# Two-layer graph network: the chain from aggregation to scores in 20 slots instead of 23

## The chip, the cores and the metric

The kernel runs on one core of one Trainium2 chip (trn2). The metric is the device time of one execution in microseconds. The kernel before took 729.9 us (median of 3 runs, 729.87 to 730.22).

## The reference

4096 nodes with 256 features and a 4096 x 4096 adjacency matrix go through two layers, each with a residual and a layer norm. The first averages neighbours and combines them with the node itself. The second scores every pair of a node and a neighbour with small tanh networks, masks the scores, takes a softmax over each row and averages values with it.

```
mask = adj > 0;  deg = mask.sum(1)
agg  = mask @ x / max(deg, 1)
out  = relu(concat(x @ W_self + b_self, agg @ W_nb + b_nb) @ W_comb + b_comb)
x1   = layernorm(x + out)
neib_att = tanh(neigh @ Wn1 + bn1) @ Wn2 + bn2
value    = neigh @ Wv + bv
x_att    = tanh(x1 @ Wx1 + bx1) @ Wx2 + bx2
ws   = softmax(where(mask, leaky_relu(x_att @ neib_att.T), NEG_BIG), axis=1)
out2 = concat(x1 @ Wfx + bfx, ws @ value)
return layernorm(x1 + out2)
```

## The kernel before

The rows are handled in 32 blocks of 128 nodes (`NB`), and the neighbours of a block in 8 groups of 512 (`NG`, `GW`). Each engine has its own instruction list, and all lists are written by one loop over slots, `for s in range(0, SLOTS + 3)`. A slot is no time but a place in the order. Block b begins its aggregation in slot 8b; `due(s, at)` says which block and group has a step with offset `at` in slot s, and `due(s, at, 0)` is for steps done once a block. Block 31 aggregates in slots 248 to 255. At any time work of five blocks is interleaved. Engines wait on each other by semaphores only.

Products are made with numbers split into a high and a low 16-bit half; so each step that feeds a matmul is a high half on ScalarE and a low half on VectorE, which subtracts.

The chain of a block, with its offset from slot 8b:

- masks (`make_mask`, VectorE, from `adj_sb`, in four quarters, at the offsets `MASK_SLOTS`), then SyncE's queue turns each quarter with a transposing DMA into `mask_t` (`turn_mask`) and loads the next block's quarter of adj (`load_adj`). `mask_t` has one buffer; the turn of a quarter waits for the aggregation of the same quarter of the block before.
- 0 to 7: `aggregate` on TensorE, one group a slot. 8: `degrees` (VectorE), `mean_of` (ScalarE). 9: `mean_transpose` (TensorE). 10: `mean_high`. 11: `mean_low`. 12: `combine` (TensorE, 12 matmuls of 256 columns). 13: `layer0` (four VectorE instructions) and `norm1` (three GpSimd ones). 15: `normalise1` gives `x1`. 16: `x1_transpose`. 17 and 18: `x1_high`, `x1_low`. 19: `hidden_and_fx`. 20: `x_tanh`, `tanh_low`. 21: `x_attention`. 22: `xatt_high`, `xatt_low`, which fill `stack`, and `add_fx`.
- 23 to 30: `scores` (TensorE, one group a slot) and `leaky` (ScalarE), one slot later `masked_scores` (VectorE). 31: `row_max`. 32 to 36: `exps`, four quarters. 33 to 38: `turn_p`, transposes of the exponentials of six groups on TensorE, each followed by `p_high` and `p_low`; the other two groups are split by `wide_high` (35) and `wide_low` (36) and turned by DMA (37). 34 to 41: `weigh_values`, 12 matmuls a slot. 42: `layer1`, then `norm2`, `normalise2` and the store.

Score matmuls use two PSUM buffers, so `scores` of a group waits for `leaky` of two groups earlier; so does `turn_p` for `p_low`. `weigh_values` of a block's first group waits for the third step of `layer1` of the block before, since `ps_v` has one buffer.

The list of SyncE has, in each slot, in this order: wide turn, mask turn with adj load, `turn_x` (offset 4), the x load (`LAYER0_AT + 1`) and the store. Slots 0 to 11 also hold the last preparations: values and attention parts of neighbour tiles 4 to 7, and splitting of x (`first_part`). After slot 255 there is no aggregation and the list drains until slot 289.

Of the kernel before, what the change touches and what calls it, by code (L numbers as in the profile page):

```python
# [50 lines left out]

MASK_SLOTS = (-7, -5, -1, 0)
MEAN_AT = 8
MEAN_T_AT = 9
MEAN_SPLIT_AT = 10
MEAN_LOW_AT = 11
X_TURN_AT = 4
COMBINE_AT = 12  # L60
LAYER0_AT = 13
X1_AT = 15
X1_T_AT = 16
X1_COPY_AT = 17
X1_LOW_AT = 18
HIDDEN_AT = 19
TANH_AT = 20
XATT_AT = 21
STACK_AT = 22
SCORE_AT = 23  # L70
ROW_MAX_AT = 31
TURN_AT = 33
WEIGH_AT = 34

# [2 lines left out]
BY_PE = NG - 2 * BY_DMA  # L79
EXPS = ((0, 1), (1, 0), (2, 2), (4, 3))  # L80
EXP_PLACE = [[quarter for _, quarter in EXPS].index(k) for k in range(4)]
WIDE_HIGH_AT = (35,)
WIDE_LOW_AT = (36,)
WIDE_TURN_AT = (37,)
WIDE_WEIGH_AT = (40,)
LAYER1_AT = 42
SLOTS = NG * (NB - 1) + LAYER1_AT + 1


# [6 lines left out]
def due(s, at, k=None):  # L96

    b, g = divmod(s - at, NG)
    return (b, g) if 0 <= b < NB and (k is None or g == k) else None
# [19 lines left out]
def gnn_kernel(nc, x, adj, w_self, b_self, w_nb, b_nb, w_comb, b_comb, neigh, wx1, bx1, wx2, bx2,  # L119
# [5 lines left out]
    with ExitStack() as ctx:  # L125
# [362 lines left out]
        def _(dve):  # L488
# [207 lines left out]
            def row_max(b):  # L696
                dve.wait_ge(score_made, NG * (b + 1))
                dve.tensor_reduce(row[:, 0:1], part_max[:, :], AX.X, ALU.max).then_inc(max_step, 1)
                dve.wait_ge(max_step, 2 * b + 1)
                at_least(dve, exp_made, NQ * (b - 1))  # L700
                dve.tensor_scalar(exp_bias[:, b % 2:b % 2 + 1], row[:, 0:1], minus_unit, EXP_SHIFT, ALU.mult,  # L701
                                  ALU.add).then_inc(max_step, 1)

            def degrees(b):
                dve.wait_ge(agg_done, NQ * (b + 1))
                at_least(dve, mean_made, b)
                dve.tensor_scalar(row[:, 4:5], ps_agg[b % 2][:, D:D + 1], EDGE_F8, x_scale, ALU.max,
                                  ALU.mult).then_inc(degree_step, 1)
                dve.wait_ge(degree_step, 2 * b + 1)
                dve.reciprocal(row[:, 5:6], row[:, 4:5]).then_inc(degree_step, 1)  # L710
# [32 lines left out]
            def xatt_low(b):  # L743
                s = slice(H, 2 * H)
                dve.wait_ge(xatt_hi, b + 1)
                dve.scalar_tensor_tensor(out=stack[s, b % 2, :], in0=ps_x[s, 0:P], scalar=bx2_sb[s, 0:1],  # L746
                                         in1=stack[s, b % 2, :], op0=ALU.add, op1=ALU.subtract).then_inc(stack_ready, 1)

            def add_fx(b):
                dve.wait_ge(resx_made, b + 1)  # L750
                dve.scalar_tensor_tensor(out=res[:, b % RES_BUFS, 0:DV], in0=ps_x[:, 3 * P:4 * P], scalar=fx_inv,
                                         in1=res[:, b % RES_BUFS, 0:DV], op0=ALU.mult, op1=ALU.add).then_inc(res_made, 1)

            def p_low(b, j, n):
                dve.wait_ge(p_hi_made, n + 1)
                dve.tensor_tensor(p_lo[:, n % 2, :], ps_t[n % 2][:, :], p_hi[:, n % 2, :],  # L756
                                  ALU.subtract).then_inc(p_lo_made, 1)
# [23 lines left out]
            for s in range(0, SLOTS + 3):  # L781
                first_part(s)
                if d := due(s, LAYER1_AT, 0):
                    layer1(d[0])
                if d := due(s, SCORE_AT + 1):
                    masked_scores(*d)
                if d := due(s, MEAN_AT, 0):
                    degrees(d[0])
                if d := due(s, MEAN_LOW_AT, 0):
                    mean_low(d[0])  # L790
                if d := due(s, X1_LOW_AT, 0):
                    x1_low(d[0])
                if d := due(s, TANH_AT, 0):
                    tanh_low(d[0])
                if d := due(s, ROW_MAX_AT, 0):
                    row_max(d[0])
                if d := due(s, LAYER0_AT, 0):
                    layer0(d[0])
                if d := due(s, STACK_AT, 0):
                    xatt_low(d[0])  # L800
                    add_fx(d[0])
                for q, at in enumerate(MASK_SLOTS):
                    if (d := due(s, at, 0)) and d[0] > 0:
                        make_mask(d[0], q)
                for w, at in enumerate(WIDE_LOW_AT):
                    if d := due(s, at, 0):
                        wide_low(d[0], w)
                if d := turned_by_pe(s, TURN_AT):
                    p_low(*d)

        @block.scalar
        def _(act):
# [61 lines left out]
            def first_part(s):  # L874
                if s == 0:
                    n_high(PRE - 1)
                if (t := turn_due(s, 0)) is not None:
                    if t + 1 < NT:
                        copy_rows_t(t + 1)
                    v_high(t)  # L880
                if (t := turn_due(s, 1)) is not None:
                    hidden(t)
                if (t := turn_due(s, 2)) is not None:
                    n_high(t)
                if s + 2 < NT:
                    x_high(s + 2)
                if s in (6, 7):
                    act.wait_ge(m_scaled, 1)
                    act.activation(m16[:, 0, s - 6, :], m_both[:, s - 6, :], ACT.Copy, scale=m_scale).then_inc(m_hi_made, 1)
# [20 lines left out]
            def exps(b, q):  # L910
                act.wait_ge(max_step, 2 * (b + 1))
                part = score[:, b % 2, q * QW:(q + 1) * QW]
                act.activation(part, part, ACT.Exp, bias=exp_bias[:, b % 2:b % 2 + 1],  # L913
                               scale=score_unit).then_inc(exp_made, 1)

            def p_high(b, j, n):
                act.wait_ge(pt_done, n + 1)

                at_least(act, pv_done, NG * b + j - 1 if j >= 2 else NG * (b - 1) + BY_PE + j - 1)
                act.copy(p_hi[:, n % 2, :], ps_t[n % 2][:, :]).then_inc(p_hi_made, 1)  # L920
# [37 lines left out]

            for s in range(0, SLOTS + 3):
                first_part(s)  # L960
                if d := due(s, MEAN_SPLIT_AT, 0):
                    mean_high(d[0])
                if d := due(s, X1_AT, 0):
                    normalise1(d[0])
                if d := due(s, X1_COPY_AT, 0):
                    x1_high(d[0])
                if d := due(s, TANH_AT, 0):
                    x_tanh(d[0])
                if d := due(s, STACK_AT, 0):
                    xatt_high(d[0])  # L970
                for at, q in EXPS:
                    if d := due(s, ROW_MAX_AT + 1 + at, 0):
                        exps(d[0], q)
                for w, at in enumerate(WIDE_HIGH_AT):
                    if d := due(s, at, 0):
                        wide_high(d[0], w)
                if d := turned_by_pe(s, TURN_AT):
                    p_high(*d)
                if d := due(s, SCORE_AT):
                    leaky(*d)  # L980
                if d := due(s, MEAN_AT, 0):
                    mean_of(d[0])
                if d := due(s, LAYER1_AT + 1, 0):
                    normalise2(d[0])

        @block.tensor
        def _(pe):
# [199 lines left out]
            for s in range(0, SLOTS + 3):  # L1187
                first_part(s)
                if d := turned_by_pe(s, TURN_AT):
                    turn_p(*d)  # L1190
                if d := due(s, 0):
                    aggregate(*d)
                if d := due(s, MEAN_T_AT, 0):
                    mean_transpose(d[0])
                if d := due(s, COMBINE_AT, 0):
                    combine(d[0])
                if d := due(s, X1_T_AT, 0):
                    x1_transpose(d[0])
                if d := due(s, HIDDEN_AT, 0):
                    hidden_and_fx(d[0])  # L1200
                if d := due(s, XATT_AT, 0):
                    x_attention(d[0])
                if d := due(s, SCORE_AT):
                    scores(*d)
                if d := turned_by_pe(s, WEIGH_AT):
                    weigh_values(*d[0:2])
                for w, at in enumerate(WIDE_WEIGH_AT):
                    if (d := due(s, at)) and d[1] < 2:
                        weigh_values(d[0], BY_PE + 2 * w + d[1])

# [1 line left out]
_INS = ['x', 'adj', 'L0_gnn_W_self', 'L0_gnn_b_self', 'L0_gnn_W_nb', 'L0_gnn_b_nb', 'L0_gnn_W_comb', 'L0_gnn_b_comb',  # L1212
# [20 lines left out]
```

## Time and profile before

| | before |
|---|---|
| median of 3 runs | 729.9 us |
| the profiled execution | 730.62 us |
| its span, first to last instruction | 728.8 us |
| TensorE busy | 689.6 us (95%) |
| VectorE busy | 621.7 us (85%) |
| ScalarE busy | 573.5 us (79%) |
| GpSimd busy | 129.9 us (18%) |
| chain that ended last, TensorE's share | 86% |
| mean granted TensorE clock | 0.994 |

Busy time counts an instruction from its start to its modelled end. Matmuls overlap, so what a matmul costs in a full queue is the distance between two starts, not its length. A line number is that of the kernel.

### The profile page before, as it was taken

The page shows a single profiled execution, that of the slowest core. Times are in us where ns is not written, and L with a number is a line of the kernel's source. Part 1 is how long each engine was busy: PE and PEld are TensorE (multiplying, and loading weights), DVE is VectorE, ACT ScalarE, POOL GpSimd, SP SyncE. Part 2 cuts the span into 40 slices and gives each one's busy share as a digit, 9 for nine tenths or more (in the row PEclk, how much of TensorE's full clock was granted, in tenths as well). Part 3 has the DMA queues.
Part 4 walks back from the last instruction along what each step waited for, and adds up shares of the span by engine and source line. Part 5 has one row for each costly group of instructions (what it writes and reads, how often), then busy time and mean ns, then how long its engine had stood idle before and what let it go on. Part 6 is the DMA issues. An engine that isn't in the chain of part 4 may idle for free.

```text
span 728.8 us, 19763 instructions
## 1 busy us (share of the span) xinstructions
PE 689.6 (95%) x7344; PEld 592.1 (81%) x7344; DVE 621.7 (85%) x1535; ACT 573.5 (79%) x920; POOL 129.9 (18%) x242
## 2 busy tenths in 40 slices
PE   5989998999999999999999999999999999998775
PEld 4646676888888888888888888888888888886554
DVE  4887668999999999999999999999999999987874
ACT  2455248888888888888888888888888888889884
POOL 0010111222211222221111222211122221111101
PEclk9989999999999999999999999999999999999999
DMA  8967999999999999999999999999999999841111
GB/s 266 370 150 165 228 269 236 195 203 223 196 202 206 223 208 202 216 224 213 220 212 208 208 203 219 188 221 205 206 200 217 212 220 217 167 81 33 39 42 44
DMA packets 260145, 141.39 MB, mean 194 GB/s; under 512 B 225361, under 2 KB 243665, under 8 KB 260049
## 3 DMA queue, kind: packets, MB, share of 16 engines
q1 hardware_dynamic: 259604, 140.10, 88.7%
q8 instruction: 59, 0.97, 0.6%
q14 instruction: 38, 0.30, 0.1%
q10 hardware_dynamic: 444, 0.02, 0.0%
HBM read 81.35 MB, written 4.19 MB: 117 GB/s over the span
## 4 chain that ended last, share of the span: by engine, by line
PE 86%; ACT 5%; DVE 4%; issue 3%; POOL 1%; DMA 1%; SPq 0%; POOLq 0%; ACTq 0%
PE ps_v L1137 22%; PE ps_agg L1092 15%; PE ps_agg L1095 14%; PE ps_t L1116 10%; PE ps_s L1107 7%; PE ps_agg L1156 3%; PE ps_agg L1159 3%; PE ps_s L1006 2%; PE ps_v L1014 2%; PE ps_x L1176 1%; PE ps_x L1179 1%; ACT score L913 1%; PE ps_t L997 1%; PE ps_x L1023 1%; DMA neigh_sb<-in_L_gnn_neigh_dram 1%
## 5 line engine op out<-in xcount | busy, mean ns | idle before, releaser
L1092 PE MATMUL ps_agg<-x,mask_t 128*128 128x257 f16 x1024 | 243.4, 274 | 0.2 <-DMA mask_t<-mask 0.2
L1095 PE MATMUL ps_agg<-x,mask_t 128*128 128x256 f16 x1024 | 237.4, 273 | 0.3 <-DVE x L533 0.3
L907 ACT ACTIVATE score<-ps_s,sc 128x512 f32<-128x512 f32 x256 | 178.7, 698 | 63.1 <-PE ps_s L1107 57.6
L692 DVE CUSTOM_DVE_ANT_0 score<-score,mask 128x512 f32<-128x512 f32 x256 | 175.9, 687 | 16.7 <-ACT score L907 14.3
L1137 PEld LDWEIGHTS ps_v<-v,late 128*128 128x128 f16 x2304 | 143.9, 97 | 41.7 <-DVE late L756 16.9
L1137 PE MATMUL ps_v<-v,late 128*128 128x129 f16 (+1 forms) x2304 | 162.6, 219 | 11.6 <-DVE late L773 6.0
L913 ACT ACTIVATE score<-score,exp_bias,sc 128x1024 f32<-128x1024 f32 x128 | 159.4, 1246 | 3.2 <-DVE exp_bias L701 3.2
L756 DVE TENSOR_TENSOR late<-ps_t,late 128x512 f16<-128x512 f32 x192 | 130.7, 681 | 33.2 <-ACT late L920 31.4
L920 ACT CAST late<-ps_t 128x512 f16<-128x512 f32 x192 | 114.8, 598 | 20.4 <-PE ps_t L1116 20.4
L1116 PE MATMUL ps_t<-ident,score 128*128 128x128 f32 x768 | 116.8, 275 | 5.3 <-ACT score L913 5.1
L1095 PEld LDWEIGHTS ps_agg<-x,mask_t 128*128 128x128 fp8e4 x1024 | 100.3, 98 | 15.5 <-issue 5.2
L1092 PEld LDWEIGHTS ps_agg<-x,mask_t 128*128 128x128 fp8e4 x1024 | 100.5, 98 | 15.1 <-issue 0.8
L1107 PE MATMUL ps_s<-n,stack 96*128 96x512 f16 x256 | 97.3, 380 | 1.0 <-DVE stack L746 0.9
L544 DVE TENSOR_SCALAR mask<-adj_sb 128x1024 bf16<-128x1024 int32 x128 | 89.8, 704 | 3.9
L1116 PEld LDWEIGHTS ps_t<-ident,score 128*128 128x128 f32 x768 | 80.9, 141 | 7.3 <-ACT score L913 7.1
L473 POOL TENSOR_SCALAR mv<-mv 128x1 f32<-128x1 f32 x32 | 18.9, 590 | 232.9 <-DVE mv L779 232.9
L1137 PEld LDWEIGHTS ps_v<-v,neigh_sb 128*128 128x128 f16 x768 | 49.0, 97 | 7.9
L1137 PE MATMUL ps_v<-v,neigh_sb 128*128 128x129 f16 (+1 forms) x768 | 54.0, 219 | 0.0
L459 POOL TENSOR_SCALAR mv<-mv 128x1 f32<-128x1 f32 x32 | 7.9, 246 | 248.9 <-DVE mv L730 248.9
L761 DVE TENSOR_TENSOR neigh_sb<-score,neigh_sb 128x1024 f16<-128x1024 f32 x32 | 39.2, 1224 | 0.9
L468 POOL TENSOR_TENSOR late<-x,bfv_sb 128x256 f32<-128x256 f32 x32 | 27.8, 868 | 45.1 <-ACT x L931 45.1
L925 ACT CAST neigh_sb<-score 128x1024 f16<-128x1024 f32 x32 | 34.8, 1087 | 0.0
(133 smaller groups left out, 805.4 us busy)
## 6 DMA issues: line engine op xcount, KB each, us to landing
adj_sb<-in_adj_dram SPq DMA_DIRECT2D x128, 512.0 KB, 5.3
neigh_sb<-in_L_gnn_neigh_dram SPq DMA_DIRECT2D x8, 512.0 KB, 8.0
score<-in_x_dram SPq DMA_DIRECT2D x8, 512.0 KB, 8.5
x_in<-in_x_dram SPq DMA_DIRECT2D x32, 128.0 KB, 2.7
out_dram<-out_sb SPq DMA_DIRECT2D x32, 128.0 KB, 3.3
mask_t<-mask SPq DMA_TRANSPOSE x128, 4.8
neigh_sb<-neigh_sb SPq DMA_TRANSPOSE x64, 3.7
mask<-in_L_gnn_W_comb_dram SPq DMA_DIRECT2D x1, 512.0 KB, 9.2
```

The source lines that it names most:

```text
L544: dve.tensor_scalar(mask[:, b % MASK_BUFS, q * QW:(q + 1) * QW], adj_sb[:, q, :], 0.0, EDGE, ALU.is_le, ALU.add).then_inc(mask_made, 1)
L692: dve.tensor_tensor_reduce(score[:, b % 2, part], score[:, b % 2, part], mask[:, b % MASK_BUFS, part], 1.0, -3.0e38, ALU.subtract, ALU.max ...
L756: dve.tensor_tensor(p_lo[:, n % 2, :], ps_t[n % 2][:, :], p_hi[:, n % 2, :], ALU.subtract).then_inc(p_lo_made, 1)
L761: dve.tensor_tensor(wide_p[:, w, 1, :], score[:, b % 2, w * QW:(w + 1) * QW], wide_p[:, w, 0, :], ALU.subtract).then_inc(wide_lo_made[w], 1)
L907: act.activation(score[:, b % 2, k * GW:(k + 1) * GW], ps_s[k % 2][:, :], ACT.Prelu, alpha=SLOPE, scale=score_scale).then_inc(leaky_made, 1)
L913: act.activation(part, part, ACT.Exp, bias=exp_bias[:, b % 2:b % 2 + 1], scale=score_unit).then_inc(exp_made, 1)
L920: act.copy(p_hi[:, n % 2, :], ps_t[n % 2][:, :]).then_inc(p_hi_made, 1)
L1092: mm = pe.matmul(agg[:, 0:D + 1], mask_t8[:, c, 0, :], x16[:, c, X_HI:X_ONE + 1], start=(c == 0), stop=(c == NC - 1), skip_group_check=True)
L1095: mm = pe.matmul(agg[:, 0:D], mask_t8[:, c, 0, :], x16[:, c, X_LO:X_LO + D], start=False, stop=False, skip_group_check=True)
L1107: pe.matmul(ps_s[k % 2][:, :], stack[:, b % 2, :], n16[:, k * GW:(k + 1) * GW], start=True, stop=True).then_inc(s_done, 1)
L1116: mm = pe.transpose(ps_t[n % 2][:, u * P:(u + 1) * P], score[:, b % 2, at:at + P], ident[:, :])
L1137: mm = pe.matmul(ps_v[:, 0:n], p, v16[:, c, v:v + n], start=(j == 0 and u == 0 and part == 0), stop=(j == NG - 1 and u == CG - 1 and part ...
```

## The change

Offsets of the chain shrink: low half of the mean 11 to 10, combine 12 to 10, layer 0 13 to 11, x1 transposes 16 to 15, copy and low half 17 and 18 to 16, hidden 19 to 17, tanh 20 to 18, x attention 21 to 18, stack 22 to 19, scores 23 to 20. All that follows the scores moves by the same three slots. The distance from the x1 halves (16) to the hidden product (17) stays one slot, and that product now comes last in its slot. Masks are made at offsets -4, -3, -2 and 0 instead of -7, -5, -1 and 0. Within a slot the order changes on three engines: TensorE does scores and weighing ahead of the chain's pieces; ScalarE does the exponentials first and `mean_of` ahead of `leaky`; VectorE does the row maximum first, `add_fx` one slot later, and `degrees` at the end of slot 7. No instruction is added or removed.

```diff
-MASK_SLOTS = (-7, -5, -1, 0)
+MASK_SLOTS = (-4, -3, -2, 0)
 MEAN_AT = 8
 MEAN_T_AT = 9
 MEAN_SPLIT_AT = 10
-MEAN_LOW_AT = 11
+MEAN_LOW_AT = 10
 X_TURN_AT = 4
-COMBINE_AT = 12
-LAYER0_AT = 13
+COMBINE_AT = 10
+LAYER0_AT = 11
 X1_AT = 15
-X1_T_AT = 16
-X1_COPY_AT = 17
-X1_LOW_AT = 18
-HIDDEN_AT = 19
-TANH_AT = 20
-XATT_AT = 21
-STACK_AT = 22
-SCORE_AT = 23
-ROW_MAX_AT = 31
-TURN_AT = 33
-WEIGH_AT = 34
+X1_T_AT = 15
+X1_COPY_AT = 16
+X1_LOW_AT = 16
+HIDDEN_AT = 17
+TANH_AT = 18
+XATT_AT = 18
+STACK_AT = 19
+SCORE_AT = 20
+ROW_MAX_AT = 28
+TURN_AT = 30
+WEIGH_AT = 31
...
-WIDE_HIGH_AT = (35,)
-WIDE_LOW_AT = (36,)
-WIDE_TURN_AT = (37,)
-WIDE_WEIGH_AT = (40,)
-LAYER1_AT = 42
+WIDE_HIGH_AT = (32,)
+WIDE_LOW_AT = (33,)
+WIDE_TURN_AT = (34,)
+WIDE_WEIGH_AT = (37,)
+LAYER1_AT = 39
...
                 if d := due(s, SCORE_AT + 1):
                     masked_scores(*d)
-                if d := due(s, MEAN_AT, 0):
-                    degrees(d[0])
+                if d := due(s, ROW_MAX_AT, 0):
+                    row_max(d[0])
...
-                if d := due(s, ROW_MAX_AT, 0):
-                    row_max(d[0])
...
                 if d := due(s, STACK_AT, 0):
                     xatt_low(d[0])
+                if d := due(s, STACK_AT + 1, 0):
                     add_fx(d[0])
...
+                if d := due(s, MEAN_AT - 1, 0):
+                    degrees(d[0])
...
                 first_part(s)
+                for at, q in EXPS:
+                    if d := due(s, ROW_MAX_AT + 1 + at, 0):
+                        exps(d[0], q)
...
-                for at, q in EXPS:
-                    if d := due(s, ROW_MAX_AT + 1 + at, 0):
-                        exps(d[0], q)
...
+                if d := due(s, MEAN_AT, 0):
+                    mean_of(d[0])
                 if d := due(s, SCORE_AT):
                     leaky(*d)
-                if d := due(s, MEAN_AT, 0):
-                    mean_of(d[0])
...
                 if d := due(s, 0):
                     aggregate(*d)
+                if d := due(s, SCORE_AT):
+                    scores(*d)
+                if d := turned_by_pe(s, WEIGH_AT):
+                    weigh_values(*d[0:2])
+                for w, at in enumerate(WIDE_WEIGH_AT):
+                    if (d := due(s, at)) and d[1] < 2:
+                        weigh_values(d[0], BY_PE + 2 * w + d[1])
                 if d := due(s, MEAN_T_AT, 0):
                     mean_transpose(d[0])
...
                     x_attention(d[0])
-                if d := due(s, SCORE_AT):
-                    scores(*d)
-                if d := turned_by_pe(s, WEIGH_AT):
-                    weigh_values(*d[0:2])
-                for w, at in enumerate(WIDE_WEIGH_AT):
-                    if (d := due(s, at)) and d[1] < 2:
-                        weigh_values(d[0], BY_PE + 2 * w + d[1])
```

## Rows read from the trace of the kernel before

**Rows 1.** Busy us by stretch, instructions in brackets, clock, DMA share, GB/s
```profile
80.00:100.00 20.00, 18.04 (x162) 15.04 (x163) 10.56 (x24) 5.16 (x11) 5.36 (x8) 1.00 1.15 238
120.00:140.00 20.00, 20.00 (x228) 17.86 (x227) 17.78 (x46) 16.84 (x29) 2.75 (x6) 1.00 0.98 212
680.00:700.00 20.00, 14.00 (x171) 11.26 (x169) 15.60 (x43) 18.70 (x29) 2.25 (x4) 1.00 0.14 35
```
**Rows 2.** TensorE in order of time, steady stretch: start, length, line, tiles, count
```profile
401.42 0.61 PE L1116 MATMUL ps_t<-ident,score 128*128 128x128 f32 x4
401.86 0.27 PE L1095 MATMUL ps_agg<-x,mask_t 128*128 128x256 f16 x1
...
402.76 0.38 PE L1107 MATMUL ps_s<-n,stack 96*128 96x512 f16 x1
402.98 0.85 PE L1137 MATMUL ps_v<-v,late 128*128 128x129 f16 x12
403.66 0.27 PE L1095 MATMUL ps_agg<-x,mask_t 128*128 128x256 f16 x1
...
411.49 0.84 PE L1137 MATMUL ps_v<-v,late 128*128 128x129 f16 x12
...
416.41 0.82 PE L1156 MATMUL ps_agg<-m,x_t 128*128 128x256 f16 x6
...
417.72 0.38 PE L1107 MATMUL ps_s<-n,stack 96*128 96x512 f16 x1
```
**Rows 3.** VectorE in order of time: head, then steady stretch
```profile
85.09 0.18 DVE L730 BATCH_NORM_AGGREGATE mv<-stat 128x2 f32<-128x6 f32 x1
...
399.98 0.48 DVE L722 SCALAR_TENSOR_TENSOR l<-ps_agg,sc,z_bias 128x256 f32<-128x256 f32 x1
...
410.99 0.35 DVE L773 SCALAR_TENSOR_TENSOR late<-ps_v,row,late 128x128 f32<-128x128 f32 x1
...
419.48 0.48 DVE L722 SCALAR_TENSOR_TENSOR l<-ps_agg,sc,z_bias 128x256 f32<-128x256 f32 x1
```
**Rows 4.** ScalarE in order of time, steady stretch
```profile
410.73 1.27 ACT L913 ACTIVATE score<-score,exp_bias,sc 128x1024 f32<-128x1024 f32 x1
411.86 0.61 ACT L920 CAST late<-ps_t 128x512 f16<-128x512 f32 x1
412.32 0.74 ACT L907 ACTIVATE score<-ps_s,sc 128x512 f32<-128x512 f32 x1
412.90 1.09 ACT L925 CAST neigh_sb<-score 128x1024 f16<-128x1024 f32 x1
```
**Rows 5.** TensorE in the head, with idle before and releaser in brackets
```profile
88.67 0.44 PE L1170 MATMUL ps_x<-ident,x 128*128 128x128 f32 x2 [1.49 <-ACT x L931]
...
98.03 0.28 PE L1092 MATMUL ps_agg<-x,mask_t 128*128 128x257 f16 x1 [0.19 <-DMA mask_t<-mask]
...
114.72 0.66 PE L1116 MATMUL ps_t<-ident,score 128*128 128x128 f32 x4 [1.05 <-ACT score L913]
```
**Rows 6.** SyncE's queue: three mask turns, then each one's us to landing
```profile
82.63 1.23 SPq L364 DMA_TRANSPOSE mask_t<-mask  x1
...
86.44 1.46 SPq L364 DMA_TRANSPOSE mask_t<-mask  x1
...
90.60 1.56 SPq L364 DMA_TRANSPOSE mask_t<-mask  x1
...
DMA to landing us min/median/max: 3.1/3.1/3.1
...
DMA to landing us min/median/max: 3.7/3.7/3.7
...
DMA to landing us min/median/max: 7.4/7.4/7.4
```
**Rows 7.** TensorE in the tail: first instructions of slots 256 and 259
```profile
658.95 0.39 PE L1170 MATMUL ps_x<-ident,x 128*128 128x128 f32 x2
...
665.36 0.61 PE L1116 MATMUL ps_t<-ident,score 128*128 128x128 f32 x4
```

## Prediction

> **What bounds the kernel now.** I read the busy time by stretch first [rows 1]. From 120 us to about 658 us TensorE is busy 20.00 us in every 20 us, VectorE 17.78 and ScalarE 16.84. Before and after that stretch TensorE has holes: 18.04 of 20 us at 80 to 100, and 14.00 of 20 us at 680 to 700, where ScalarE is the busiest engine (18.70).
>
> The second view is TensorE's work in order of time inside that stretch [rows 2]. It shows a slot piece by piece, by the starts: four transposes of the exponentials 0.44 us (401.42 to 401.86), aggregation 0.90 (to 402.76), score matmul 0.22 (to 402.98), weighing of values 0.68 (to 403.66, where the next slot begins). A slot with transposes takes 2.24 us, one without 1.80. Pieces of the chain come on top: the combine matmuls 1.31 us (416.41 to 417.72), and, from the same view, the two transposes 0.22 each and the hidden and fx matmuls 0.67. Six slots with and two without transposes, plus 2.48 for the chain, are 19.5 us a block. The same VectorE instruction of two blocks following one another stands at 399.98 and 419.48 [rows 3], so a block takes 19.50 us: TensorE's queue is full, and no order of slots can shorten this stretch, since the change removes no instruction. Only the two ends can give or take.
>
> The Trainium skill, page Perfetto Trace Analysis, section Identifying the Most-Contended Engine, says that matmul busy time isn't a good measure of TensorE's headroom and that the busy share of weight loads is one. By that share (17.86 of 20 us [rows 1]) a tenth of the steady stretch would be open, some 50 us. The starts in [rows 2] follow one another without a gap, so here the rows decide, and I give that headroom nothing.
>
> **The change, part by part.**
>
> 1. The tail. The aggregation's last slot is slot 255 in both kernels. Before, scores of the last block start 23 slots after its first aggregation slot and its last weighing is in slot 289; after, in slot 286. So the new tail from slot 256 does what the old one did from slot 259, with the end of the chain pushed in. Old slot 256 begins at 658.95 and old slot 259 at 665.36 [rows 7]: 6.41 us of tail disappear. What comes into the shorter tail from the chain (scaling of the last mean, a copy of x1, a split: about 0.36 us each on ScalarE by their starts) falls where ScalarE and VectorE still have their lag of the steady slots. Laid out slot by slot with the starts of [rows 4] (exponential 1.13 from 410.73 to 411.86, high half 0.47, score copy 0.58; wide copy 1.09 long, 0.94 to the next start) the new slots 256 to 261 take 13.5 us, and the old 259 to 264 took 13.6 (665.36 to 678.97). I count nothing for it, with 0.5 us either way. Gain: 6.4.
>
> 2. What was taken out of the tail must be done before slot 256: three more slots of score, transposes and weighing lie beside an aggregation. Three slots with their chain pieces in the full stretch cost 2.0 + 2.45 + 2.24 = 6.7 us by [rows 2], against the 6.4 us of tail. This is -0.3, so parts 1 and 2 together are worth nothing unless the kernel reaches the full stretch earlier. Old slot 33, the first with transposes of exponentials, begins at 114.72 [rows 5]; the new kernel's counterpart is slot 30. The gain is 114.72 minus the start of new slot 30, minus 0.3.
>
> 3. The head, which fixes that start. The old head has waits of 0.28 (combine of block 0), 1.49 for x1, 0.19 for a mask, 0.65, 0.89, 0.47, and 1.05 for the first exponentials; the three that matter stand in [rows 5]. A head slot is only 0.9 to 1.1 us long, so three slots fewer hide 3 us less latency.
>  - Block 0: combine goes from slot 12 to slot 10. ScalarE copies the mean at 78.6 and VectorE can subtract at 79.1, so combine begins at 79.6 after a wait of 0.8; the old one began at 82.15. But VectorE has the last neighbour part ahead of the layer-0 arithmetic in slot 11, and that follows an aggregation piece on TensorE: layer 0 ends at 85.1, as before (85.09 + 0.18 [rows 3]).
>  - Masks of block 2: they move from slots 9, 11, 15, 16 to 12, 13, 14, 16. On VectorE the first one now stands behind layer 0 of block 0, so it is made at 85.8. The queue is then empty and it lands 3.1 us on, as did the turn issued at 82.63 [rows 6], at 88.9. Slot 16 of the new kernel needs it at 87.7 to 88.6. Nothing is lost to speak of.
>  - SyncE's queue: mask 0, its load, the turned x and the x load now all come ahead of mask 1. In the old order the same four stand between the turns of 82.63 and 86.44, 3.8 us. Mask 1 is then issued at 89.6 and lands 3.7 later (the turn of 86.44), at 93.3. TensorE has slots 16 and 17 with the hidden matmuls done at 91.6: a wait of 1.7.
>  - With aggregation, combine 1.31 and slot 19, slot 20 begins at 96.5, just as mask 2 lands; masks and loads follow one another every 2.8 to 3.2 us in this stretch (landings worked out from issue plus time to land), so mask 3 lands at 99.5 to 100.5, a wait of about 1.2 in slot 22. A turn in a crowded queue took 7.4 (issued 90.60 [rows 6]).
>  - Block 3 in the same manner: first aggregation at 102.8, its second mask 1.4 late at 107.3, slots 26 to 29 end at 113.1. The first exponentials come 3.1 us after the block's last score, at 113.8. Slot 30 begins at 113.9.
>  The gain is then 114.72 - 113.9 - 0.3 = 0.5, with 0.2 more from slot 5, where the aggregation waits 0.28 for a half of x that stood behind masks no longer made in slots 1 and 3. Parts 1 to 3 together: 0.7 faster.
>
> 4. The steady stretch after the change. Per block the slots get other companions. TensorE's longest neighbours are slots 1 (mean transposes, hidden: 3.1 us) and 2 (combine: 3.6 us). I followed ScalarE through the block by [rows 4]: from the first exponentials in slot 5 it works without a pause until slot 2 and falls at most 1.2 us behind. Its closest dates: x1 is ready 0.36 us before its transposes; the last exponentials 0.6 before theirs; the mean's halves 0.6 before combine. VectorE's layer-1 step is ready 0.46 before the weighing that waits for it; in the old kernel it ends at 411.34 and the weighing begins at 411.49 [rows 2, 3], 0.15. Mask 0 has 4 slots instead of 7: made at 13.7 us of the block, needed at 19.9, and an empty queue takes 3.1. All have room, so this stretch costs 0. Score matmuls and weighing standing ahead of the chain's matmuls removes nothing either. Moving row maximum, exponentials and degrees within their slots is nothing as long as these dates hold; if one is missed, it is missed in each of 28 blocks.
>
> The clock: at 680 to 700 TensorE was idle 6 of 20 us, in pieces, and the granted clock stayed at 1.00, the 2.4 GHz level [rows 1]. The new head has waits of 1 to 2 us, as long as the 1.49 of [rows 5], after which the clock also stood. The Trainium skill, TensorE: Matmul & The Clock Gate, part 1, says that an idle TensorE is put back to half its clock; the pieces here are short, and by rows nothing is due.
>
> **Sum.** Own time of the profiled execution 730.62, of which 728.8 is span; 730.62 + 0.3 - 0.8 - 0.2 = 729.9. The runs shown have a median of 729.9, 0.7 below the profiled one: 729.2. A difference of 0.2% (1.5 us) is about what can be told from no change.
>
> **Rivals.**
> - The head gives more than I grant (for: the transfers stood idle before 85.8, so the queue may drain faster than 2.8 us a mask; x1 of block 0 may come a whole 1.2 us earlier, since one of the small GpSimd steps took unusually long; against: four transfers now stand in one row). With mask waits of 0.5 instead of 1.2 to 1.7 slot 30 begins at 112.0: 114.72 - 112.0 - 0.3 = 2.4 faster, 727.5.
> - The head loses more: the masks of blocks 2 and 3, in three slots in a row, land as the crowded one did (7.4 instead of 3.7 [rows 6]) and slot 30 begins at 117. That is 117 - 114.72 + 0.3 = 2.6 slower: 732.5. It decides from slot 30 beginning later than 116.
> - One of the dates in part 4 is missed in each block, most likely x1's or the layer-1 step. Against it: 0.36 and 0.46 us of room. At 0.1 us in each of 28 blocks it is 2.8 us, 732.0; at 0.3 it is 737.6.
> - The clock falls in the head after one of the new waits. The price: head work that now takes 4 us (aggregation and scores, [rows 2]) takes 8 at 1.2 GHz, of which a part falls into waits; 3 us, 732.2.
> - That the change doesn't shorten the chain: excluded, all of the slot numbers are constants of the code.
>
> **Chances.** Forecast 0.40 (728.5 to 731.3); more from the head 0.34; less from it 0.14; missed dates 0.09; clock 0.03. Faster 0.34, same 0.40, slower 0.26. The range takes in the second case to 727.0 and the third and the small form of the fourth to 733.5.
>
> **What would show it.** Period between two layer-0 steps 19.50 us: part 4 right. Last aggregation's slot to the end 63.5 us instead of 69.9: part 1. Start of the first transposes of exponentials: 113.9 in part 3, 112 or 117 in the rivals; waits for mask transfers in TensorE's list for blocks 2 and 3, 3 to 5 us in all. The forecast is wrong if the period moves by 0.1, or if the first transposes start outside of 112.5 to 115.5.

## The result, and the profile after

The changed kernel took 732.17 us in the median of 10 runs (729.24 to 734.32), the kernel before 730.05 (729.43 to 731.44): a ratio of 1.0026, 95% interval 1.0015 to 1.0036. It is slower by a quarter of a per cent, about 2 us, and its runs spread over 5 us where those of before spread over 2. Run again on another chip it took 730.81 (729.12 to 733.02), ratio 1.0011, 1.0001 to 1.0021. The profiled execution took 731.15 us, with a span of 729.3 (before: 730.62 and 728.8).

Three numbers of the profile say where the forecast held. First, busy time by stretch, to set beside [rows 1] (TensorE, weight loads, VectorE, ScalarE, GpSimd, then granted clock, DMA share and GB/s):

```profile
80.00:100.00 20.00, 17.12 (x131) 12.75 (x130) 10.94 (x27) 5.04 (x10) 4.53 (x7) 0.91 0.75 174
120.00:140.00 20.00, 20.00 (x228) 17.92 (x227) 18.53 (x47) 16.85 (x29) 4.71 (x7) 1.00 1.04 218
...
320.00:340.00 20.00, 18.60 (x211) 16.48 (x209) 16.90 (x44) 15.53 (x26) 4.71 (x7) 1.00 1.18 194
...
500.00:520.00 20.00, 19.41 (x221) 17.17 (x219) 17.61 (x45) 16.48 (x27) 4.71 (x7) 1.00 0.97 216
```

TensorE is full again from 120 us on, but for short waits that the kernel before doesn't have. TensorE's list in order of time, idle before an instruction in brackets:

```profile
112.76 0.66 PE L1117 MATMUL ps_t<-ident,score 128*128 128x128 f32 x4 [0.97 <-ACT score L914]
...
328.16 0.86 PE L1138 MATMUL ps_v<-v,neigh_sb 128*128 128x129 f16 x12 [1.40 <-DMA neigh_sb<-neigh_sb]
...
504.53 0.86 PE L1138 MATMUL ps_v<-v,neigh_sb 128*128 128x129 f16 x12 [0.59 <-DMA neigh_sb<-neigh_sb]
...
666.00 0.60 PE L1117 MATMUL ps_t<-ident,score 128*128 128x128 f32 x4
```

- The first transposes of exponentials come at 112.76, two us ahead of 114.72 [rows 5].
- Slot 256 begins its transposes at 666.00, and 63.3 us are left; before, 63.4 us were left from 665.36 on [rows 7]. The tail is three slots shorter, as worked out.
- Between the two lie 553.24 us; before, from 114.72 to 665.36, 550.64. Of the 2.6 us more, 0.3 are the three denser slots. The rest, 2.3, is what two blocks lose to waits for `neigh_sb<-neigh_sb`, the wide turn by DMA, of which the kernel before had none.

The block's period, from the starts of the mean's transposes, is 19.50 or 19.51 us in 25 of 27 blocks of the steady stretch to within 0.05; the two others are 21.07 (from 316.96 to 338.03) and 20.27. SyncE's queue and the landing of its wide turns (min, median, max over the 64, first of before, then of after):

```profile
DMA to landing us min/median/max: 2.7/3.7/5.3
```
```profile
DMA to landing us min/median/max: 2.7/5.6/8.5
```

SyncE's list of the changed kernel, one block (start, length of the issue):

```profile
405.85 1.23 SPq L364 DMA_TRANSPOSE mask_t<-mask  x1
407.13 0.59 SPq L359 DMA_DIRECT2D adj_sb<-in_adj_dram  x1
407.81 1.19 SPq L370 DMA_TRANSPOSE x_t<-x  x1
409.05 0.60 SPq L380 DMA_DIRECT2D x_in<-in_x_dram  x1
409.75 1.41 SPq L364 DMA_TRANSPOSE mask_t<-mask  x1
411.20 0.59 SPq L359 DMA_DIRECT2D adj_sb<-in_adj_dram  x1
411.88 1.24 SPq L364 DMA_TRANSPOSE mask_t<-mask  x1
413.16 1.00 SPq L359 DMA_DIRECT2D adj_sb<-in_adj_dram  x1
414.26 1.71 SPq L364 DMA_TRANSPOSE mask_t<-mask  x1
416.02 0.58 SPq L359 DMA_DIRECT2D adj_sb<-in_adj_dram  x1
416.64 0.44 SPq L384 DMA_DIRECT2D out_dram<-out_sb  x1
417.17 4.54 SPq L376 DMA_TRANSPOSE neigh_sb<-neigh_sb  x2
```

In the kernel before, the queue has a gap between 413.6 and 415.24, and behind it only one mask turn with its load, the turned x and the store stand ahead of the wide turn:

```profile
413.01 0.58 SPq L359 DMA_DIRECT2D adj_sb<-in_adj_dram  x1
415.24 1.23 SPq L364 DMA_TRANSPOSE mask_t<-mask  x1
416.52 0.72 SPq L359 DMA_DIRECT2D adj_sb<-in_adj_dram  x1
417.33 1.19 SPq L370 DMA_TRANSPOSE x_t<-x  x1
418.57 0.58 SPq L384 DMA_DIRECT2D out_dram<-out_sb  x1
419.25 2.85 SPq L376 DMA_TRANSPOSE neigh_sb<-neigh_sb  x2
```

This is the reading of the case. In the changed kernel the queue issues from 405.85 to 421.7 with hardly a pause, and the wide turn, two transposing DMAs, is the last of it, behind four mask turns and four adj loads (and the turned x, the x load and the store). From the issue of its first half to the landing of its second it takes 7.5 us in the median of the steady blocks, against 4.9 before. The weighing that needs both halves starts 1.06 us after the second has landed in the median, against 1.63 before, and in 5 of 26 blocks within 0.1 us, in none before. So the date was close already, and now it is missed at times: in the block of 328.16 the second half was issued at 319.65 and landed after 8.5 us, at 328.15.

### The profile page after: what moved, and what is told of

It reads as the page before. It is cut to its first block, busy times and chain, and to the rows that moved or that the text cites. A ratio compares the mean times of both kernels' runs of the same rounds, so it can differ in the third digit from the quotient of the medians.

```text
span 729.3 us, 19763 instructions
## 1 busy us (share of the span) xinstructions
PE 691.2 (95%) x7344; PEld 593.8 (81%) x7344; DVE 622.5 (85%) x1535; ACT 564.8 (77%) x920; POOL 152.7 (21%) x242
## 4 chain that ended last, share of the span: by engine, by line
PE 80%; ACT 6%; DVE 4%; issue 4%; DMA 4%; SPq 2%; POOL 1%; ACTq 0%; POOLq 0%; DVEq 0%
PE ps_v L1138 20%; PE ps_agg L1093 14%; PE ps_agg L1096 14%; PE ps_t L1117 10%; PE ps_s L1108 6%; PE ps_agg L1157 3%; PE ps_agg L1160 3%; DMA neigh_sb<-neigh_sb 2%; PE ps_v L1015 2%; ACT score L914 2%; PE ps_s L1007 2%; PE ps_x L1180 1%; PE ps_x L1177 1%; PE ps_t L998 1%; ACT late L921 1%
## 5 line engine op out<-in xcount | busy, mean ns | idle before, releaser
L1138 PEld LDWEIGHTS ps_v<-v,late 128*128 128x128 f16 x2304 | 145.6, 97 | 39.1 <-DVE late L756 15.8
L756 DVE TENSOR_TENSOR late<-ps_t,late 128x512 f16<-128x512 f32 x192 | 132.4, 690 | 30.9 <-ACT late L921 27.6
L544 DVE TENSOR_SCALAR mask<-adj_sb 128x1024 bf16<-128x1024 int32 x128 | 87.2, 684 | 0.0
L468 POOL TENSOR_TENSOR late<-x,bfv_sb 128x256 f32<-128x256 f32 x32 | 31.3, 977 | 197.3 <-ACT x L932 197.3
L459 POOL TENSOR_SCALAR mv<-mv 128x1 f32<-128x1 f32 x32 | 8.0, 250 | 270.1 <-DVE mv L730 270.1
L475 POOL TENSOR_TENSOR mv<-mv,minus_half 128x1 f32<-128x1 f32 x32 | 48.4, 1512 | 2.7
L957 ACT ACTIVATE stack<-ps_x,bx_sb 96x128 f16<-96x128 f32 x32 | 11.6, 363 | 40.9 <-PE ps_x L1186 40.9
```

Of the source, the lines that this page charges most:

```text
L475: pool.tensor_tensor(mv2[:, 3:4], mv2[:, 2:3], minus_half[:, :], ALU.pow).then_inc(norm2_step, 1)
L544: dve.tensor_scalar(mask[:, b % MASK_BUFS, q * QW:(q + 1) * QW], adj_sb[:, q, :], 0.0, EDGE, ALU.is_le, ALU.add).then_inc(mask_made, 1)
L1138: mm = pe.matmul(ps_v[:, 0:n], p, v16[:, c, v:v + n], start=(j == 0 and u == 0 and part == 0), stop=(j == NG - 1 and u == CG - 1 and part ...
```

## The experiments

All ratios are to runs of the kernel before on the same chip. The theory after the result was this: the wide turn is late because of what stands ahead of it in SyncE's queue.

**e3 and e4: a load left out.** From block 2 on the adj load of one quarter is left out, so masks of that quarter are made from block 1's data; e3 (below) leaves out the last quarter's, e4 the same with `q != 1` and `q == 1`, the second's.

```diff
-                        if d[0] + 1 < NB:
+                        if d[0] + 1 < NB and q != 3:
                             load_adj(d[0] + 1, q)
...
-                dve.wait_ge(adj_in[q], 16 * (b + 1))
+                dve.wait_ge(adj_in[q], 16 * (min(b, 1) + 1 if q == 3 else b + 1))
```

> The changed kernel without the adj loads of the last quarter from block 2 on (masks of that quarter are made from block 1's data), which are the loads issued just ahead of the wide turn. Theory (queue ahead of the wide turn): landing falls to 4 us, no waits, 727.5 to 729.5. Rival (total DMA load): the same gain as without the second quarter's load.

> The changed kernel without the adj loads of the second quarter from block 2 on, in slot 5, far from the wide turn in slot 2. Theory (queue ahead of the wide turn): a wide turn still stands behind the last quarter's turn and load, landing stays above 5 us in the median and waits stay, 730 to 733. Rival (total DMA load): less traffic anywhere helps alike, 727.5 to 729.5.

Measured, without the last quarter's load: 729.17 us, ratio 0.9989 (0.9981 to 0.9998); every steady block 19.50 or 19.51, no wait for the wide turn. Without the second quarter's: 729.80 us, 0.9998 (0.9989 to 1.0006), which lies between the two ranges expected for it; one block of 20.88. The landings of the wide turn from 120 to 660 us, the last quarter's load left out, then the second's:

```profile
DMA to landing us min/median/max: 2.7/4.4/6.3
```
```profile
DMA to landing us min/median/max: 2.7/5.6/8.7
```

With the load away that stands just ahead of it, the wide turn lands 1.4 us earlier in the median (5.8 in the changed kernel over the same stretch). With a load of the same size away three slots earlier it lands as late as ever. Yet there were fewer waits in that run too, so the rival may have a part in it (less traffic would start the whole row of issues earlier; the runs do not separate that). With the waits gone, e3 is 0.8 us below the kernel before by the ratio, about what the prediction had forecast for a stretch without waits.

**e1: the last quarter a slot earlier.**

```diff
-MASK_SLOTS = (-4, -3, -2, 0)
+MASK_SLOTS = (-4, -3, -2, -1)
```

> The changed kernel with the last mask quarter one slot earlier (offsets -4, -3, -2, -1). Theory (queue ahead of the wide turn): the wide turn of slot 2 no longer stands right behind the last mask turn and its adj load, so its halves land 3.5 to 5 us after issue instead of 5.6 in the median, TensorE's waits for them (2.0 us in the profiled execution of the changed kernel, more in most others) vanish, and with the head's 2 us kept the kernel takes 727 to 729 us, 1 to 3 below the kernel before, with little spread. Rival (four mask turns in a row simply crowd the queue, the place of the last one does not matter): as the changed kernel, 730.5 to 734.

Measured: 733.03 us, 1.0043 (1.0031 to 1.0055). The theory's number is missed by 4 us, and both reasons stand in the profile. Its SyncE list:

```profile
413.12 1.65 SPq L359 DMA_DIRECT2D adj_sb<-in_adj_dram  x1
414.87 1.77 SPq L364 DMA_TRANSPOSE mask_t<-mask  x1
416.68 0.58 SPq L359 DMA_DIRECT2D adj_sb<-in_adj_dram  x1
417.30 0.43 SPq L384 DMA_DIRECT2D out_dram<-out_sb  x1
417.83 5.07 SPq L376 DMA_TRANSPOSE neigh_sb<-neigh_sb  x2
```

The queue was never waiting for the last mask; it was still busy with those before it. A slot number alone moved nothing in it, and the landing stayed at 5.6 in the median. And who waited for whom from 130 to 650 us (sum, times, longest):

```profile
PEld ps_v L1138 <- DVE late L756: 9.0, 27, 0.3
PEld ps_v L1138 <- DMA neigh_sb<-neigh_sb: 2.4, 6, 0.7
```

The mask now stands in another slot of VectorE, and by the first line a low half of the exponentials (`late` of L756) is late for TensorE once in each of 27 blocks. A block takes 19.62 us instead of 19.51, which is 3 us in all.

**e2: new chain, old mask offsets.**

```diff
-MASK_SLOTS = (-4, -3, -2, 0)
+MASK_SLOTS = (-7, -5, -1, 0)
```

> The changed kernel with the old mask offsets (-7, -5, -1, 0). Theory (queue ahead of the wide turn): slots 0 and 1 now both hold a mask turn and a load directly ahead of the wide turn in slot 2, so the waits of TensorE for the wide turn grow to 1 us or more in many blocks, 735 to 750 us. Rival (three mask turns in three slots in a row are what crowds the queue): spread out they crowd nothing, waits vanish, 727 to 729.5.

Measured: 783.23 us, 1.0726 (1.0688 to 1.0763), blocks of 20.4 to 24.7 us.

```profile
PEld ps_v L1138 <- DVE late L756: 33.6, 72, 0.6
PEld ps_v L1138 <- DMA neigh_sb<-neigh_sb: 29.1, 21, 3.1
```

The direction is that of the theory, the size is above it. The waits for the wide turn are there, and a second lot as large from VectorE, whose slot 1 now has the wide low half and a mask. The new mask offsets were needed by the new chain.

**e5: old chain, new mask offsets.** The kernel before with one line of the change.

```diff
-MASK_SLOTS = (-7, -5, -1, 0)
+MASK_SLOTS = (-4, -3, -2, 0)
```

> The kernel before with the new mask offsets alone (-4, -3, -2, 0), its wide turn in slot 5 of a block's eight, right between mask turns of slots 4, 5 and 6. Theory (what stands ahead of the wide turn decides): ahead of it stand only one mask turn, its load, the turned x and the store; in the kernel before there were two mask turns within four slots. VectorE now makes the second mask in slot 5, beside layer 0, its second-longest slot. Waits for the wide turn in a few blocks at most, 730 to 733 us. Rival (three mask turns in a row crowd the queue wherever the wide turn stands): waits in most blocks, 735 or more.

Measured: 761.29 us, 1.042 (1.0404 to 1.0435); both theories had the main cause wrong. What is late most of all is VectorE, with two masks in its slots 4 and 5:

```profile
PEld ps_v L1137 <- DVE late L756: 34.7, 50, 1.0
PEld ps_v L1137 <- DMA neigh_sb<-neigh_sb: 7.7, 11, 1.9
```

There are waits for the wide turn too, in 11 blocks, though it lands in 3.9 us in the median: it is issued 2.8 us after its low half was made, against 1.5 in the kernel before (medians), behind a mask turn that now belongs to slot 4 instead of 3.

**e6: the last quarter behind the wide turn.** Now the order in the queue is changed, not only a date.

```diff
-MASK_SLOTS = (-4, -3, -2, 0)
+MASK_SLOTS = (-4, -3, -2, 2)
```

> The changed kernel with the last mask quarter made in slot 2 (offset +2), so that its turn and load stand behind the wide turn in SyncE's queue and VectorE makes it in a light slot. Theory (queue ahead of the wide turn): the wide halves land 3 to 4 us after issue, no block of the steady stretch is longer than 19.51 us; the head may lose 1 to 2 us to the late quarter, 727.5 to 730.5. Rival (the total DMA load of the queue at that time): waits stay, 731 to 734.

Measured: 728.86 us (728.15 to 729.75), 0.9983 (0.9974 to 0.9992). Its SyncE list and the landings from 120 to 660 us:

```profile
412.98 0.34 SPq L384 DMA_DIRECT2D out_dram<-out_sb  x1
414.37 2.58 SPq L376 DMA_TRANSPOSE neigh_sb<-neigh_sb  x2
417.36 1.24 SPq L364 DMA_TRANSPOSE mask_t<-mask  x1
```
```profile
DMA to landing us min/median/max: 2.7/4.1/6.4
```

All the same transfers are made; the wide turn lands in 4.1 instead of 5.8 us after its issue, and every steady block takes 19.50 or 19.51 us. The edit also moves a mask on VectorE, but this isn't what helps: the wide low half, for which the wide turn waits, ends 0.46 us after the mean's transposes begin in both kernels (medians of the blocks from 200 to 600 us). In e6 the turn is issued 0.03 us after that, in the changed kernel 0.80 after it, and the second half lands 5.7 instead of 8.7 us after those transposes. This settles the cause of the steady stretch's loss: it is the place of the wide turn in the queue, and not a date on VectorE; the full number of transfers costs nothing once the order is right.

By the ratios (0.9983 against 1.0026 and 1.0011 for the changed kernel) the order of one mask turn with its load and the wide turn is worth 2 to 3 us. The head gives none of it: from block 0's mean transposes to slot 30 it takes 38.46 us (73.70 to 112.16), and in the two profiles of the changed kernel 37.99 and 37.81. The Trainium skill, DMA: Bandwidth & Descriptors, section Queues, rings and completion order, says that on each DMA engine the descriptors of a queue are consumed in ring order. The changed kernel's trace agrees: in the block from 405.85 on every transfer lands in the order of its issue, the last quarter's load at 421.44, the store at 421.84, the two halves of the wide turn at 422.84 and 423.73.

**e7 and e8: old offsets for blocks 1 to 3.** A helper picks the offsets by block; e7 leaves the later ones at (-4, -3, -2, 0), e8 takes (-4, -3, -2, 2).

```diff
+EARLY_MASK_SLOTS = (-7, -5, -1, 0)
+MASK_SLOTS = (-4, -3, -2, 2)
...
+def mask_due(s, q):
+    for slots, blocks in ((EARLY_MASK_SLOTS, range(1, 4)), (MASK_SLOTS, range(4, NB))):
+        if (d := due(s, slots[q], 0)) and d[0] in blocks:
+            return d
+    return None
```

> The changed kernel with the old mask offsets for blocks 1 to 3 only. It asks what the later masks cost in the head. By the working of the prediction the masks of blocks 2 and 3 hold back TensorE 1 to 3 us before slot 30: the transposes of the mean of block 3 then come 1.5 to 3 us earlier than in the changed kernel's profile (121.9), the waits for the wide turn stay as in the changed kernel: 728.5 to 732. Rival (the head is bound by the first exponentials and not by masks): no difference from the changed kernel.

> Both edits: old offsets for blocks 1 to 3, then (-4, -3, -2, 2). Theory: steady blocks of 19.51 us without waits and the shorter head: 726 to 728.5, faster than the kernel before by 1.5 to 4 us. If the waits for the wide turn come from the total load, 730 to 732.

e7: 729.13 us, 0.9988 (0.9979 to 0.9997), the waits for the wide turn still there, the transposes of the mean of block 3 at 119.35 instead of 121.89. e8: 726.87 us (726.74 to 727.42), 0.9956 (0.9944 to 0.9969), 3.2 us below the kernel before and faster than both. TensorE's head in e8 (idle before and its releaser in brackets):

```profile
97.22 0.28 PE L1104 MATMUL ps_agg<-x,mask_t 128*128 128x256 f16 x1 [0.77 <-DMA mask_t<-mask]
...
110.81 0.66 PE L1125 MATMUL ps_t<-ident,score 128*128 128x128 f32 x4 [0.97 <-ACT score L922]
```

One mask wait of 0.77 us is left of those of blocks 2 and 3, and the first transposes of exponentials begin at 110.81, 1.95 us ahead of the changed kernel's 112.76. The steady stretch keeps its 19.51 us a block. So the two edits add up: the order in the queue pays in the steady stretch, the early masks in the head.

**e9 and e10: the order within a slot.** Both start from e6. In e9 TensorE's chain pieces stand ahead of scores and weighing again; in e10 ScalarE's exponentials stand behind its chain pieces and `mean_of` behind `leaky`, as in the kernel before.

```diff
                     aggregate(*d)
-                if d := due(s, SCORE_AT):
-                    scores(*d)
-                if d := turned_by_pe(s, WEIGH_AT):
-                    weigh_values(*d[0:2])
...
                     x_attention(d[0])
+                if d := due(s, SCORE_AT):
+                    scores(*d)
+                if d := turned_by_pe(s, WEIGH_AT):
+                    weigh_values(*d[0:2])
```
```diff
                 first_part(s)
-                for at, q in EXPS:
-                    if d := due(s, ROW_MAX_AT + 1 + at, 0):
-                        exps(d[0], q)
...
                     xatt_high(d[0])
+                for at, q in EXPS:
+                    if d := due(s, ROW_MAX_AT + 1 + at, 0):
+                        exps(d[0], q)
...
-                if d := due(s, MEAN_AT, 0):
-                    mean_of(d[0])
                 if d := due(s, SCORE_AT):
                     leaky(*d)
+                if d := due(s, MEAN_AT, 0):
+                    mean_of(d[0])
```

> The kernel of e6 (changed kernel, last mask quarter at +2) with TensorE's chain pieces ahead of scores and weighing again, as in the kernel before. The prediction gave the new order within the slot no cost and no gain. Theory (the order is what makes combine possible in slot 10): by the dates of the prediction the low half of the mean is ready at 26.1 to 26.4 us of the block's clock, and combine would then be wanted at 26.1, so each block waits 0.2 to 0.5 us, and score matmuls stand behind it: blocks of 19.6 to 20.0 us, 732 to 742 us. Rival (order in the slot is free): blocks of 19.51 us, as e6, 728 to 730.

> The kernel of e6 with ScalarE's order within the slot as before: exponentials behind the chain's pieces, mean_of behind leaky. Theory: only slot 7 (offset 31) has both an exponential and the scaling of x1, so x1 comes 1.1 us earlier and its last exponentials stay where they are, and no date is missed: blocks of 19.51 us, 728 to 730 us. Rival: the exponentials' place is what keeps TensorE fed, blocks longer than 19.6 us, over 732.

e9: 766.50 us, 1.0504 (1.0491 to 1.0518). Blocks take 20.63 us, 1.12 more. The list of waits:

```profile
PEld ps_x L1171 <- ACT x L932: 19.5, 25, 0.8
PEld ps_v L1138 <- DVE late L756: 13.1, 26, 0.5
```

The time expected for it, 742 us at most, is missed by 24. It isn't combine that is late but x1, and by the second line low halves of the exponentials: x1's transposes are wanted some 0.9 us earlier in slot 15 (score matmul 0.22 and weighing 0.68 [rows 2] stood ahead of them), and the prediction had given that date 0.36 us. e10: 729.07 us, 0.9986 (0.9977 to 0.9995), blocks of 19.51 and no waits: ScalarE's order is free in this kernel.

**e11: the changed kernel once more.**

> The changed kernel as it is, a second profiled execution. Theory (queue ahead of the wide turn): most blocks of the steady stretch 19.51 us, a few longer by 0.1 to 2 us, other ones than in the first profile, each with a wait for the wide turn; the sum of what they are over makes the run's time, 729 to 734.5. Rival (the loss is a fixed one of certain blocks): the same blocks are long.

The waits for the wide turn from 130 to 650 us, in the first profile of the changed kernel and then in this one (sum, times, longest):

```profile
PEld ps_v L1138 <- DMA neigh_sb<-neigh_sb: 3.6, 6, 1.8
```
```profile
PEld ps_v L1138 <- DMA neigh_sb<-neigh_sb: 4.1, 8, 1.0
```

Its profiled execution (730.11 us) has seven blocks over 19.55 us in the steady stretch, the longest 20.24, and none of them is one of the two long ones of the first profile. What they are over 19.51 comes to 2.4 us; in the first it was 2.3 (21.07 and 20.27 against 19.51). So many blocks are close to the edge (a median of 0.66 us from landing to weighing here, 1.06 there), and which ones fall over it changes from one execution to the next. That fits with the wider spread of the changed kernel's runs (729.12 to 733.02 here, 728.15 to 729.75 for e6).

## Why the prediction was wrong, point by point

- *The steady stretch is full and its period 19.50 us*: right, to 0.01 us, wherever no DMA is waited for.
- *The tail loses 6.4 us and the stretch gains 6.7*: right. 63.3 us are left from slot 256 on (63.5 foreseen), and of the 2.6 us between the two lines above 0.3 remain when the waits' 2.3 are taken off.
- *The head, slot 30 at 113.9*: 112.76 (e11: 111.72), so the 0.8 us by which it was to come before 114.72 were 2.0 (e11: 3.0). Most of the difference lies ahead of the steps that the working shortened. Block 0's mean transposes, which stand in slot 9 in both kernels, began at 75.75 in the kernel before, but at 74.77 in the changed one and at 73.91 in e11. Of these 1.0 and 1.8 us, 0.28 is the wait for a half of x in slot 5, which the prediction counted apart; where the rest comes from no run separates, and in the other profiles of kernels made from the changed one this step lies anywhere from 73.70 to 75.25. From there to slot 30 it takes 37.99 us (e11: 37.81) against 38.97 before, 1.0 and 1.2 less where 0.8 was forecast. Inside the head the terms moved more: x1's wait was 1.90 us, the later mask waits 0.73 and 0.37 where the working had 1.2 and 1.4 (in e11 1.39 and 1.46, where it had 1.7 and 1.2, and none in block 3). That masks were the bound in the head was right: with old offsets for three blocks (e7, e8) slot 30 begins at 110.2 and 110.8.
- *The clock*: the rival with a chance of 0.03 came true in the first profile, and cost next to nothing. After x1's wait of 1.90 us the granted clock fell to 0.50, that is 1.2 GHz, and matmuls of 256 columns start 0.21 us apart instead of 0.11:

```profile
88.00:90.00 2.00, 2.00 (x11) 1.35 (x11) 1.02 (x2) 0.75 (x2) 0.42 (x1) 0.50 1.05 267
90.00:92.00 2.00, 2.00 (x17) 1.61 (x16) 0.00 (x0) 0.14 (x1) 0.00 (x0) 0.65 1.21 241
```

 In e11 the clock stayed at 1.00 after the same wait. TensorE then waited 1.39 us for the first mask that the slow aggregation of the first profile didn't wait for, and 1.46 instead of 0.73 for the next one. From x1's transposes to slot 30 it took 25.09 us with the clock down (87.67 to 112.76) and 24.90 without (86.82 to 111.72). So in this pair the price, 3 us by the rival's sum, lay under the mask waits but for 0.2 us. The statement that by rows nothing is due, since 1.49 us of waiting had left the clock alone, was too sure.
- *"All have room, so this stretch costs 0" (part 4)*: this step failed. It listed x1, the last exponentials, the mean's halves, the layer-1 step and mask 0, and gave the other DMA that TensorE waits for, the wide turn, no date at all. The order of SyncE's list would have shown that a date was due: with the old offsets one mask turn and its load come right ahead of the wide turn, behind a gap in the queue, and with the new ones all four mask turns and their loads. The missing term is 2.3 and 2.4 us in the two profiles. With it and the head as measured the sum for a profiled execution, 729.9, in which the head and slot 5 had 1.0 together, becomes 729.9 + 2.3 - 1.0 = 731.2 for the first (731.15 measured), and 729.9 + 2.4 - 2.0 = 730.3 for e11 (730.11 measured). What is left between forecast and result is the step from a profile to the median: 0.7 off for the kernel before, but 1.0 on for the changed kernel's first runs and 0.7 on for e11's, since its waits differ from execution to execution. That e11's median of 730.81 is inside of the forecast's 728.5 to 731.3 is luck: the head's early start hides part of the waits. The rival of a missed date had the right form (a little in some blocks, 732.0) but the wrong place.
- *Scores and weighing ahead of the chain's matmuls remove nothing*: true of the period as it stands, wrong as a statement on the edit. Without it each block costs 1.12 us more (e9). The margin of x1 of 0.36 us holds only with that order.
- *Mask 0 with 4 slots has room*: right, no steady block waited for a mask.
- *The chain's 2.48 us in a block*: the pieces named come to 2.42 (1.31 + 0.22 + 0.22 + 0.67). Nothing hangs on it, since the period was read from the rows as 19.50.

## What to carry to other kernels

Where one queue carries transfers with different deadlines, a slot number is only the earliest time of an issue; what decides is the order in the queue, and a queue that issues without a pause (as SyncE's from 405.85 to 421.7) turns a date moved by one slot into nothing, and an order changed by one place into 2 to 3 us. When steps are moved past each other, write down a date for every wait of the full engine, the DMA ones too, before giving the steady part a zero. A pipeline made three slots shorter pays only the difference between its empty slots at both ends, since the full engine must do the same work: here 6.4 us of tail for 6.7 us of filled slots.

## What the runs showed of the hardware

The same wait of TensorE for x1, 1.89 to 1.91 us, was followed by half the clock in two executions (the changed kernel's first and e3, granted clock 0.50) and by the full clock in five (e4, e6, e9, e10, e11, 1.00); in e1 a wait of 2.09 was followed by the full clock as well. The Trainium skill, TensorE: Matmul & The Clock Gate, section Part 1: The HAM clock gate, says that an idle TensorE is put back to half its clock. Two of these eight executions went that way and six didn't, so the wait's length alone doesn't tell.

GpSimd's power step of the second norm took 0.57 us in the kernel before and 1.67 in the changed one, with the same operands; two other small steps became shorter (0.77 to 0.27 and 0.61 to 0.22), one longer (0.27 to 0.77):

```profile
L475 POOL TENSOR_TENSOR mv<-mv,minus_half 128x1 f32<-128x1 f32 x27 | 15.4, 569 | 2.3
```
```profile
L475 POOL TENSOR_TENSOR mv<-mv,minus_half 128x1 f32<-128x1 f32 x27 | 45.0, 1666 | 2.2
```

The first line is of the kernel before, the second of the changed one, both from 120 to 660 us (busy us in all, mean ns of one, idle before). Spans of this engine are rough, and nothing waited for the step. In e6 it took a third length:

```profile
L475 POOL TENSOR_TENSOR mv<-mv,minus_half 128x1 f32<-128x1 f32 x27 | 30.0, 1111 | 2.2
```

The length goes with what VectorE does beside the step, in all thirteen profiles and in every steady block of each. In the five with 1.67 us (the changed kernel, e3, e4, e7, e11) VectorE works on `masked_scores`, `x1_low` and `make_mask` in that time; in the three with 1.1 (e6, e8, e9) on the first two alone; in the five with 0.57 (the kernel before, e1, e2, e5, e10) on `p_low`, beside `x1_low` at its start or `degrees` at its end. No run was made to test this, and which of these instructions holds GpSimd up, and by what, stays open.

The changed kernel lost more in its first set of runs (1.0026, interval 1.0015 to 1.0036) than in its second on another chip (1.0011, 1.0001 to 1.0021). The intervals overlap and both profiled executions have nearly the same waits, so whether there is a difference at all is open.
